# Normalising P and splitting it into f16 halves in two parts of eight heads, each turned by a transposing DMA of its own

## The chip, the cores and the metric

The kernel runs on one core of a Trainium2 chip. The metric is the device time of one execution in microseconds (us), lower is better, and the time of a kernel is the median of its runs. The engines are called PE (TensorE), DVE (VectorE), ACT (ScalarE), POOL (GpSimd) and SP (SyncE, which here only issues DMAs). They run side by side, each through its own list of instructions in order, and wait for each other through semaphores.

## What is computed

The input `x` is 64 sequences of 64 tokens with 512 features, with one condition vector of 512 per sequence. Four layers are added to it one after the other. The first is the one that the change touches:

```python
xn = _rms_norm(x, g_norm) * (1.0 + scale) + shift
q, k, v = split(xn @ W_qkv)                   # 16 heads of 32
q, k = _rms_norm(q, g_q), _rms_norm(k, g_k)
logits = jnp.einsum('bhqd,bhkd->bhqk', q, k) * d ** (-0.5)
attn = jax.nn.softmax(logits, axis=-1)        # this is P
o = jnp.einsum('bhqk,bhkd->bhqd', attn, v)
x = x + o + o @ W_out
```

The second layer samples `x` at 512 positions given by the condition (two taps with weights), the third is a GRU over the 64 tokens, the fourth an oscillator (four Runge-Kutta steps for each token) driven by the result.

## The kernel before, in words

The kernel has two stages. The first, attention and sampling, takes about 620 us, the second, the two recurrences side by side, the rest. The change is in the first stage alone.

**The slots.** The 64 sequences are taken in 32 pairs, so that the 128 tokens of a pair fill the 128 partitions. A software pipeline runs over slots `i = 0 to 31`: in slot i PE projects pair i to q, k and v (`project(p, 0)`, `(p, 1)` and `(p, 2)`, L1163), makes the scores of pair i-1 (`scores`, L1187), multiplies P with V for pair i-2 (`mix`, L1241) and projects that with `W_out` (`proj`, L1253), samples pair i-3 (`sample`, L1205) and turns the input of pair i+2 (L1262, L1264). A slot on PE starts with `turn_qk` (L1141). The order of every engine's work is written by hand in a function `slot` of its own; there is no scheduler.

**The way of P.** The scores of a pair lie in PSUM as 128 queries by 16 heads by 64 keys. In the slot after its projection a pair goes through these steps:

1. DVE takes the row minimum `mn` (L841), ACT makes 16 exponentials into `S`, one for each head, each with its row sum into `den` (`exps`, L515, 128x64 each).
2. DVE inverts the sums (`invert_sum`, L860: `rden` from `den`).
3. POOL multiplies `S` with `rden` (`norm_p`, L432, 128x1024).
4. ACT writes the high f16 half of `S` into `halves` (`high_halves`), POOL the rest as the low half (`low_halves`, L437). `halves` is a view of the tensor `front`, and the trace shows it under that name.
5. SP issues one transposing DMA from `halves` to `PT` (`turn_p`, L317), keys on the partitions.
6. `mix` in PE's next slot waits for it (`pt_in`).

The first two pairs make their exponentials in one instruction. The last two pairs, N1 and N0, are turned by PE instead of a DMA (L1173), after the same `invert_sum` and `norm_p`.

**What stands around it.** On DVE `invert_sum` stands behind `scale_qk` (L824, `qn`) and two of the eight `build` instructions of a slot (L795, `room<-rows,lidx`: an f16 compare that makes a selection matrix for `sample`), and ahead of `residual` (L888), `low_v` (L830), two `weigh_taps` (L863) and `low_wr` (L909). On ACT the order is `exps`, `high_v` (`Vt<-psQ`), `high_wr` (`Whh<-room` or `room<-room`, in most slots), `high_halves`. On POOL `norm_p` and `low_halves` end the slot, and the next one begins with `modulate` (L453, twice). On SP the transposing DMA is followed by the loads of x and of a row (L285, L289). In the trace buffer numbers are left out, so `first4` of the code is `first`. A helper `a` records all of ACT's work, so its line is L515 throughout.

## Time and profile before

| | us |
|---|---|
| median of 3 runs | 1564.39 |
| lowest and highest | 1557.45 and 1566.65 |
| the profiled execution | 1563.98 |
| its span, the part that the trace covers | 1562.2 |
| first stage, start of the span to the last sampling | about 632 |

Slots are given by their start on PE, which is the start of `turn_qk`. From 107.45 us, when the pipeline is full, to 581.09 us there are 26 of them, and they take 473.64 us. A busy time of an engine counts an instruction from its start to its end, so that an instruction that is held up by something inside the chip counts as busy while it is held.

### The profile page before, as it was taken

The numbers are of one execution on the slowest core, as the hardware profiler recorded it, in microseconds if no ns is written. First come the engines' busy times: TensorE is split into PE (matmuls) and PEld (weight loads), VectorE is DVE, ScalarE is ACT, GpSimd is POOL, SyncE is SP. The second block draws the span as 40 slices with busy tenths as digits, with TensorE's granted clock in tenths as the row PEclk, the third lists the DMA queues.
The fourth block names the chain that finished last, engine by engine and source line by source line (L and its number), as shares of the span: only waits on it lengthen the run. The fifth ranks groups of instructions, "written<-read, shape, count | busy, mean of one in ns | idle before, by whom it ended". The sixth has DMA issues, their size and how long they took to land.

```text
span 1562.2 us, 95585 instructions
## 1 busy us (share of the span) xinstructions
PE 1497.6 (96%) x42219; PEld 1327.1 (85%) x42219; DVE 1363.3 (87%) x3259; ACT 942.4 (60%) x2854; POOL 750.1 (48%) x887
## 2 busy tenths in 40 slices
PE   6899999999999999899999999999999999999995
PEld 3467776666667767899999999999999999999995
DVE  7889889888888889498888989988999889988997
ACT  6667777767777764355555555555555555555553
POOL 2566666666666665443433343433434343434331
PEclk8999999999999999999999999999999999999996
DMA  6333333444444434000000000000000000000000
GB/s 226 57 81 95 88 84 83 96 101 100 103 109 100 83 65 130 10 12 15 15 13 14 15 15 13 13 15 15 14 13 15 15 15 13 13 15 14 14 13 15
DMA packets 169054, 75.56 MB, mean 48 GB/s; under 512 B 139768, under 2 KB 154272, under 8 KB 168640
## 3 DMA queue, kind: packets, MB, share of 16 engines
q1 hardware_dynamic: 168544, 69.44, 19.4%
q8 instruction: 331, 5.42, 1.5%
q14 instruction: 83, 0.68, 0.1%
q10 hardware_dynamic: 96, 0.02, 0.0%
HBM read 33.71 MB, written 11.60 MB: 29 GB/s over the span
## 4 chain that ended last, share of the span: by engine, by line
PE 82%; DVE 5%; ACT 4%; issue 3%; POOL 3%; DMA 2%; ACTq 0%; POOLq 0%; DVEq 0%
PE psB L1472 34%; PE psA L1501 15%; PE psQ L1163 10%; PE psA L1506 7%; PE psQ L1205 6%; PE psO L1253 4%; DMA PT<-front 2%; ACT S L515 2%; PE psO L1241 2%; PE psB L1187 1%; PE psA L1141 1%; POOL S L432 1%; POOL front L437 1%; ACT front L515 1%; DVE room L795 1%
## 5 line engine op out<-in xcount | busy, mean ns | idle before, releaser
L1472 PE MATMUL psB<-first,Wx 128*128 128x64 f16 x9216 | 293.5, 194 | 5.5 <-POOL first L1784 3.8
L1501 PE MATMUL psA<-ts,Cp 128*128 128x64 f16 x8160 | 283.8, 194 | 10.3 <-ACT ts L1539 10.0
L1472 PE MATMUL psB<-first,Whh 128*128 128x64 f16 x9072 | 286.4, 193 | 0.8
L1472 PEld LDWEIGHTS psB<-first,Wx 128*128 128x128 f16 x9216 | 280.7, 98 | 6.7 <-POOL first L1784 3.9
L1163 PE MATMUL psQ<-Wx,front 128*128 128x512 f16 x1152 | 269.4, 384 | 6.3 <-DVE front L970 4.1
L1472 PEld LDWEIGHTS psB<-first,Whh 128*128 128x128 f16 x9072 | 273.8, 98 | 1.6 <-issue 1.6
L1539 ACT ACTIVATE ts<-qst 128x256 f16<-128x256 f32 x192 | 80.1, 417 | 313.9 <-DVE qst L1643 313.9
L1501 PEld LDWEIGHTS psA<-ts,Cp 128*128 128x128 f16 x8160 | 258.7, 99 | 11.5 <-ACT ts L1539 11.0
L1163 PEld LDWEIGHTS psQ<-Wx,front 128*128 128x128 f16 x1152 | 108.8, 99 | 126.7 <-issue 8.1
L1780 POOL TENSOR_TENSOR en<-rz,dn 128x256 f32<-128x256 f32 x64 | 46.8, 731 | 255.8 <-issue 255.6
L1506 PE MATMUL psA<-ts,Cp 128*128 128x64 f16 x4080 | 163.4, 194 | 0.7 <-issue 0.2
L795 DVE TENSOR_SCALAR room<-rows,lidx 128x512 f16<-128x512 f16 x256 | 158.0, 659 | 0.2 <-issue 0.2
L1506 PEld LDWEIGHTS psA<-ts,Cp 128*128 128x128 f16 x4080 | 138.6, 99 | 1.4 <-issue 1.2
L432 POOL TENSOR_TENSOR S<-S,rden 128x1024 f32<-128x1024 f32 x32 | 61.0, 1905 | 157.6 <-DVE rden L860 157.6
L1670 DVE TENSOR_TENSOR ts<-psA,ts 128x256 f16<-128x256 f32 x255 | 107.1, 420 | 31.7 <-ACT psA L1539 26.3
L515 ACT ACTIVATE S<-psB,mn 128x64 f32<-128x64 f32 x448 | 133.2, 338 | 0.6 <-DVE mn L841 0.4
L1643 DVE SCALAR_TENSOR_TENSOR rest<-cub,psQ 128x256 f32<-128x256 f32 x256 | 106.3, 415 | 7.0 <-DVE cub L1674 0.5
L1780 POOL TENSOR_TENSOR V<-X3b,first 128x256 f32<-128x256 f32 x64 | 47.0, 735 | 134.1 <-DVE first L1764 133.9
L1205 PE MATMUL psQ<-x,room 128*128 128x128 f16 x1856 | 108.5, 219 | 0.0
L1643 DVE SCALAR_TENSOR_TENSOR psO<-qst,psO 128x256 f32<-128x256 f32 x256 | 106.5, 416 | 0.0
L1205 PEld LDWEIGHTS psQ<-x,room 128*128 128x128 f16 x1856 | 104.9, 98 | 0.2
L515 ACT ACTIVATION_READ_ACCUMULATOR S<-psB,mn 128x1 f32 x448 | 104.0, 232 | 0.0
(201 smaller groups left out, 3001.0 us busy)
## 6 DMA issues: line engine op xcount, KB each, us to landing
front<-in_x SPq DMA_DIRECT2D x32, 256.0 KB, 4.6
rows<-rows_dram SPq DMA_DIRECT2D x64, 128.0 KB, 3.1
out<-ot SPq DMA_DIRECT2D x512, 16.0 KB, 1.8
x<-x SPq DMA_DIRECT2D x29, 224.0 KB
Whh<-in_L_cond_W_qkv SPq DMA_DIRECT2D x12, 256.0 KB, 7.2
room<-in_L_cond_W_hh SPq DMA_DIRECT2D x12, 256.0 KB, 2.7
room<-in_L_cond_W_ih SPq DMA_DIRECT2D x12, 256.0 KB, 2.8
wih_dram<-room SPq DMA_DIRECT2D x12, 256.0 KB, 3.2
```

Of the source, the lines that this page charges most:

```text
L432: nc.gpsimd.tensor_tensor(S[:, :, :], S[:, :, :], rden[:, :].unsqueeze(2).broadcast_to([PART, HEADS, T]), ALU.mult)\
L515: return nc.scalar.activation(out, in_, f, **k)
L795: e = v.tensor_scalar(E_of(p, b)[:, k, :], rows[b][:, :], lidx[:, k:k + 1], None, ALU.is_equal)
L1163: last = mm(psQ[:, n, :], xn[p.u][:, i, c, :], Wqkv[:, j, c, n * D:(n + 1) * D], start=(c == 0 and t == 0), stop=(c == KC - 1 and t == 2))
L1205: last = mm(o[:, m, :, :], E_of(p, b)[:, c, m * PART:(m + 1) * PART], x1_of(p)[:, :, i, c, b, :], start=(c == 0 and i == 0), stop=(c == KC ...
L1472: last = mm(o, W_[:, i, c, g * PART:(g + 1) * PART], src[:, j, c, :], start=False, stop=False, skip_group_check=True)
L1501: mm(psF[:, s % 2, m, :], Cp[:, i, c, m * PART:(m + 1) * PART], ts_[:, 0, c, :], start=(c == 0 and m == 0 and i == 0), stop=False, skip_gr ...
L1506: last = mm(psF[:, s % 2, m, :], Cp[:, 0, c, m * PART:(m + 1) * PART], ts_[:, 1, c, :], start=False, stop=(c == KC - 1), skip_group_check= ...
L1539: return nc.scalar.activation(out, in_, f, **k)
L1643: return v.scalar_tensor_tensor(out=flat(out), in0=flat(in0), scalar=scalar, in1=flat(in1), op0=ALU.mult, op1=op1)
L1670: v.tensor_tensor(ts_[:, 1, :, :], th, ts_[:, 0, :, :], ALU.subtract).then_inc(S["ts_ready"], 1)
L1780: return nc.gpsimd.tensor_tensor(flat(out), flat(in0), flat(in1), op)
```

## The change

`S`, `halves` and `PT` are treated as two parts of eight heads (h = 0 and 1). `halves` and `PT` are laid out part by part, so that one part is contiguous in each partition, and `mix` reads the new layout. Each of `norm_p`, `low_halves`, `high_halves`, `invert_sum` and `turn_p` becomes two instructions of half the width, with two counts of its semaphore for each pair in place of one. A new semaphore `exp_half` is counted up by the eighth exponential. On DVE the inversion of the first eight sums moves ahead of the last two `build` instructions and waits for `exp_half`; on ACT the first part's `high_halves` moves ahead of `high_v`. The number of matmuls stays.

```diff
         def turn_p(p, h):
-            sp.wait_ge(pl_done, p.n + 1)
+            sp.wait_ge(pl_done, p.n * 2 + h + 1)
             need(sp, mix_done, p.n)
-            sp.dma_start_transpose(PT[:, :, :, :].rearrange("p i j n -> p (i j) n"), halves.rearrange("p i s k -> p (i s k)"))\
+            sp.dma_start_transpose(PT[:, h, :, :, :].rearrange("p i j n -> p (i j) n"), halves[:, h, :, :, :].rearrange("p i s k -> p (i s k)"))\
                 .then_inc(pt_in, 16)
...
         def norm_p(p):
-            pool.wait_ge(rden_done, p.n + 1)
-            nc.gpsimd.tensor_tensor(S[:, :, :], S[:, :, :], rden[:, :].unsqueeze(2).broadcast_to([PART, HEADS, T]), ALU.mult)\
-                .then_inc(p_done, 1)
+            for h in range(2):
+                pool.wait_ge(rden_done, p.n * 2 + h + 1)
+                part = S[:, 8 * h:8 * h + 8, :]
+                nc.gpsimd.tensor_tensor(part, part, rden[:, 8 * h:8 * h + 8].unsqueeze(2).broadcast_to([PART, HEADS // 2, T]), ALU.mult)\
+                    .then_inc(p_done, 1)
...
         def low_halves(p):
-            pool.wait_ge(ph_done, p.n + 1)
-            nc.gpsimd.tensor_tensor(halves[:, 1, :, :], S[:, :, :], halves[:, 0, :, :], ALU.subtract).then_inc(pl_done, 1)
+            for h in range(2):
+                pool.wait_ge(ph_done, p.n * 2 + h + 1)
+                nc.gpsimd.tensor_tensor(halves[:, h, 1, :, :], S[:, 8 * h:8 * h + 8, :], halves[:, h, 0, :, :], ALU.subtract).then_inc(pl_done, 1)
...
-        def high_halves(p):
-            act.wait_ge(p_done, p.n + 1)
-            need(act, pt_in, p.n * 16)
-            a(halves[:, 0, :, :], S[:, :, :]).then_inc(ph_done, 1)
+        def high_halves(p, h):
+            act.wait_ge(p_done, p.n * 2 + h + 1)
+            need(act, pt_in, p.n * 32)
+            a(halves[:, h, 0, :, :], S[:, 8 * h:8 * h + 8, :]).then_inc(ph_done, 1)
...
-        def invert_sum(p):
-            dve.wait_ge(exp_done, p.n + 1)
-            need(dve, p_done, p.n)
-            v.reciprocal(rden[:, :], den[:, :]).then_inc(rden_done, 1)
+        def invert_sum(p, h):
+            if h == 0 and p.n in range(2, N1.n):
+                dve.wait_ge(exp_half, p.n - 1)
+            else:
+                dve.wait_ge(exp_done, p.n + 1)
+            need(dve, p_done, p.n * 2)
+            v.reciprocal(rden[:, 8 * h:8 * h + 8], den[:, 8 * h:8 * h + 8]).then_inc(rden_done, 1)
...
             if p := pair(-1):
                 if p.n < 2:
                     sum_p(p)
-                invert_sum(p)
+                    invert_sum(p, 0)
+                invert_sum(p, 1)
```

DVE, the end of a slot before (`room1` is the matrix that `build` writes, `XR` the running x):

```order
231 L824 TENSOR_TENSOR qn<-psQ,rs 128x512 [waits qk_T,rs_step]
232 L824 TENSOR_TENSOR qn<-psQ,rs 128x512
233 L795 TENSOR_SCALAR room1<-rows1,lidx 128x512 x2
234 L860 RECIPROCAL rden<-den 128x16 [waits p_done,exp_done]
235 L888 SCALAR_TENSOR_TENSOR XR<-psO,XR 128x4x64 [waits xT_kept,proj_done]
```

And now:

```order
238 L833 TENSOR_TENSOR qn<-psQ,rs 128x512 [waits qk_T,rs_step]
239 L833 TENSOR_TENSOR qn<-psQ,rs 128x512
240 L872 RECIPROCAL rden<-den 128x8 [waits p_done,exp_half]
241 L804 TENSOR_SCALAR room1<-rows1,lidx 128x512 x2
242 L872 RECIPROCAL rden<-den 128x8 [waits p_done,exp_done]
243 L900 SCALAR_TENSOR_TENSOR XR<-psO,XR 128x4x64 [waits xT_kept,proj_done]
```

The first reciprocal now stands ahead of the two compares, with a wait for the first eight exponentials only; the second stands where the one stood.

ACT, from the exponentials to the end of a slot before (`Whh` is `high_wr`'s target, `front<-S` is `high_halves`):

```order
125 L515 ACTIVATE S,den<-psB,mn 128x64 [waits pl_done,mn_done]
126 L515 ACTIVATE S,den<-psB,mn 128x64 x13
127 L515 ACTIVATE Vt0<-psQ 128x512 [waits mix_done,qkv_done]
128 L515 ACTIVATE Whh<-room0 128x512 [waits wr_in0]
129 L515 ACTIVATE front<-S 128x1024 [waits pt_in,p_done]
130 L515 ACTIVATE rsB<-psB 128x128 [waits xr_done,xy_T]
```

And now:

```order
126 L519 ACTIVATE S,den<-psB,mn 128x64 [waits pl_done,mn_done]
127 L519 ACTIVATE S,den<-psB,mn 128x64 x13
128 L519 ACTIVATE front<-S 128x512 [waits pt_in,p_done]
129 L519 ACTIVATE Vt0<-psQ 128x512 [waits mix_done,qkv_done]
130 L519 ACTIVATE Whh<-room0 128x512 [waits wr_in0]
131 L519 ACTIVATE front<-S 128x512 [waits pt_in,p_done]
132 L519 ACTIVATE rsB<-psB 128x128 [waits xr_done,xy_T]
```

The first part's copy moved ahead of `Vt` and `Whh`, and the wait for POOL (`p_done`) moved with it.

## Rows read from the trace of the kernel before

**Rows 1.** The page, busy time of each engine over the span.
```profile
PE 1497.6 (96%) x42219; PEld 1327.1 (85%) x42219; DVE 1363.3 (87%) x3259; ACT 942.4 (60%) x2854; POOL 750.1 (48%) x887
```

**Rows 2.** Length; busy us PE, PEld, DVE, ACT, POOL; clock; DMA: 12 long slots.
```profile
125.14:143.53 18.39, 18.10 (x356) 12.83 (x355) 17.31 (x29) 13.46 (x50) 12.95 (x12) 1.00 0.36 89
...
sum 223.56, PE 214.54 PEld 153.53 DVE 202.83 ACT 161.84 POOL 152.85; mean PE 17.88 PEld 12.79 DVE 16.90 ACT 13.49 POOL 12.74
```

**Rows 3.** The same view, the 14 short slots: the first, and the sum.
```profile
107.45:125.14 17.69, 17.63 (x355) 12.77 (x354) 14.99 (x29) 13.50 (x50) 11.28 (x11) 1.00 0.36 92
...
sum 250.08, PE 247.55 PEld 177.99 DVE 215.23 ACT 187.80 POOL 161.43; mean PE 17.68 PEld 12.71 DVE 15.37 ACT 13.41 POOL 11.53
```

**Rows 4.** Waits, 60 to 600 us: waiter, releaser, us in total, times, longest.
```profile
DVE rden L860 <- ACT S L515: 25.0, 28, 1.4
...
PE psO L1241 <- DMA PT<-front: 5.4, 6, 1.6
...
PE psQ L1163 <- issue: 2.1, 2, 1.1
```

**Rows 5.** PE in order of time, a long slot: start, us, idle before.
```profile
406.47 1.20 PE L1241 MATMUL psO<-PT,Vt 64*32 64x64 f16 x96 [1.01 <-DMA PT<-front]
```

**Rows 6.** SP in order of time: two of the 30 transposing DMAs.
```profile
308.89 1.89 SPq L317 DMA_TRANSPOSE PT<-front  x1
...
400.36 2.72 SPq L317 DMA_TRANSPOSE PT<-front  x1
```

**Rows 7.** Line L317: from issue to landing, all 30.
```profile
DMA to landing us min/median/max: 4.3/4.7/6.1
```

**Rows 8.** DMA, 308 to 316 us in 40 slices of 0.2 us: busy tenths, GB/s.
```profile
DMA  0000000000299999999999999776423322322000
GB/s 0 0 0 0 0 0 0 0 0 0 55 212 225 210 204 214 219 219 216 218 216 183 253 255 184 195 266 246 143 67 108 97 72 97 108 97 87 5 0 0
```

**Rows 9.** POOL in order of time, 303 to 318 us.
```profile
303.65 1.90 POOL L432 TENSOR_TENSOR S<-S,rden 128x1024 f32<-128x1024 f32 x1 [5.08 <-DVE rden L860]
306.73 2.13 POOL L437 TENSOR_TENSOR front<-S,front 128x1024 f16<-128x1024 f32 x1 [1.17 <-ACT front L515]
308.82 1.09 POOL L453 TENSOR_TENSOR front<-front,modA 128x512 f32<-128x512 f32 x1
...
315.98 1.15 POOL L460 TENSOR_TENSOR front<-front 128x512 f16<-128x512 f32 x1
```

**Rows 10.** ACT in order of time, the last two exponentials and what follows.
```profile
302.52 0.38 ACT L515 ACTIVATE S<-psB,mn 128x64 f32<-128x64 f32 x1
...
302.81 0.39 ACT L515 ACTIVATE S<-psB,mn 128x64 f32<-128x64 f32 x1
...
303.10 0.68 ACT L515 ACTIVATE Vt<-psQ 128x512 f16<-128x512 f32 x1
303.58 0.72 ACT L515 ACTIVATE Whh<-room 128x512 f16<-128x512 f32 x1
305.59 1.06 ACT L515 ACTIVATE front<-S 128x1024 f16<-128x1024 f32 x1 [1.29 <-POOL S L432]
```

**Rows 11.** DVE in order of time, around the same pair's sums.
```profile
301.54 0.60 DVE L795 TENSOR_SCALAR room<-rows,lidx 128x512 f16<-128x512 f16 x2
303.32 0.25 DVE L860 RECIPROCAL rden<-den 128x16 f32<-128x16 f32 x1 [1.18 <-ACT S L515]
...
307.81 1.19 DVE L795 TENSOR_SCALAR room<-rows,lidx 128x512 f16<-128x512 f16 x1
```

**Rows 12.** DVE in order of time, the slot after.
```profile
320.77 0.25 DVE L860 RECIPROCAL rden<-den 128x16 f32<-128x16 f32 x1 [0.22 <-ACT S L515]
...
326.13 0.34 DVE L795 TENSOR_SCALAR room<-rows,lidx 128x512 f16<-128x512 f16 x1
```

**Rows 13.** The chain that ended last, 600 to 612 us.
```profile
605.58 0.27 DVE rden L860
...
605.92 1.91 POOL S L432
```

More of the change, by code:

```diff
@@ L143, in attention_and_sampling @@
     rsB = sb("rsB", [PART, PART])
-    halves = front[:, 2:4, :].rearrange("p v n -> p (v n)").bitcast(F16).rearrange("p (i s k) -> p i s k", i=2, k=T)
+    halves = front[:, 2:4, :].rearrange("p v n -> p (v n)").bitcast(F16).rearrange("p (h i s k) -> p h i s k", h=2, i=2, k=T)
     xa = front[:, 4, :].rearrange("p (c b t) -> p c b t", c=KC, b=2)
@@ L157, in attention_and_sampling @@
     rden = sb("rden", [PART, HEADS])
[L158 removed]
+    PT = sb("PT", [PART, 2, 2, KC, PART], F16)
     oT = sb("oT", [PART, 2, KC, PART], F16)
@@ L336, in slot @@
             if p := pair(-2):
-                turn_p(p)
+                turn_p(p, 0)
+                turn_p(p, 1)
             if p := pair(3):
@@ L606, in exps @@
                       accum_out=den[:, s:s + 1])
+                if s == HEADS // 2 - 1:
+                    e.then_inc(exp_half, 1)
             if hi == HEADS:
@@ L688, in slot @@
                     exps(p, 2, HEADS)
+                    high_halves(p, 0)
                 else:
@@ L698, in slot @@
             if p := pair(-1):
-                high_halves(p)
+                if p.n < 2:
+                    high_halves(p, 0)
+                high_halves(p, 1)
         act.wait_ge(cond_T, 1)
@@ L1030, in slot @@
                 low_cp(0)
+            if (p := pair(-1)) and p.n > 1:
+                invert_sum(p, 0)
             if tap:
@@ L1035, in slot @@
                     sum_p(p)
-                invert_sum(p)
+                    invert_sum(p, 0)
+                invert_sum(p, 1)
             if p := pair(-2):
@@ L1095, in _ @@
         sum_p(N1)
-        invert_sum(N1)
+        invert_sum(N1, 0)
+        invert_sum(N1, 1)
         residual(N2)
@@ L1104, in _ @@
         sum_p(N0)
-        invert_sum(N0)
+        invert_sum(N0, 0)
+        invert_sum(N0, 1)
         low_o(N1)
@@ L1167, in turn_p @@
         def turn_p(p):
-            pe.wait_ge(p_done, p.n + 1)
+            pe.wait_ge(p_done, p.n * 2 + 2)
             need(pe, qk_ready, NP)
@@ L1228, in mix @@
                 if p.n <= N2.n:
-                    pe.wait_ge(pt_in, 16 * (p.n + 1))
+                    pe.wait_ge(pt_in, 32 * (p.n + 1))
                 else:
@@ L1242, in mix @@
                                   Vt[p.u][rows_, i, h * DH:(h + 1) * DH],
-                                  PT[rows_, k, r // 2 * KC + c, (r % 2) * T:(r % 2 + 1) * T], start=(t == 0), stop=(t == 2))
+                                  PT[rows_, r // 2, k, c, (r % 2) * T:(r % 2 + 1) * T], start=(t == 0), stop=(t == 2))
             last.then_inc(mix_done if b else mix0_done, 1)
```

15 lines of the change are left out of this document (7 added, 8 removed).

## The prediction

> **What bounds the kernel now.** I read the page first: PE is busy 96% of the span and DVE 87% [rows 1], so PE is the bound and DVE stands close behind. The change can only shorten the time by what PE loses around it, so the next view is the busy time by stretch, one stretch for each slot on PE. It shows two kinds of slot that mostly alternate. Fourteen short ones take 250.08 us, 17.86 on average, with PE busy in 17.68 of it; the best, at 17.69, has no hole worth the name [rows 3]. Twelve long ones take 223.56 us, 18.63 on average [rows 2]. The reader should look at DVE's column: 16.90 us in a long slot against 15.37 in a short one, and POOL's, 12.74 against 11.53, for the same instructions. TensorE's granted clock is 1.00 in these rows, its upper level, so the clock plays no part in the difference. Against 26 slots at 17.69 (459.9), the 473.64 us hold 13.7 us that PE loses. The list of waits names 5.4 us of loss as PE waiting for the transposing DMA, six times, at most 1.6 us each [rows 4]; 1.6 of it is in the slot that starts at 66 us, before the 26, and 3.8 in them. A wait of 1.01 us in a long slot is shown in [rows 5]; its DMA was issued at 400.36 [rows 6] and `mix` started 6.1 later, the longest landing of the 30 [rows 7].
>
> Why long and short? POOL and DVE tell it. In the slot that starts at 288.84 the inversion runs at 303.32, after 1.18 us of waiting for ACT's exponentials [rows 11]; POOL then multiplies 303.65 to 305.55, ACT makes the high half 305.59 to 306.65, POOL the low half 306.73 to 308.86 [rows 9, 10], and the DMA goes at 308.89 [rows 6]. The next slot began at 306.70, so POOL's low half runs into it: DVE's compare of 307.81 lasts 1.19 us and ends when POOL's does [rows 11], while the same compare in the slot after takes 0.34 [rows 12]. Late P in one slot thus makes the next one long, through DVE. The Trainium skill, page "SBUF — State Buffer", section "SBUF: two separate sides", says that DVE in its fast modes and GpSimd take a shared port pair as an exclusive lock for a whole instruction; the 1.19 against 0.34 agrees.
>
> **The change part by part.** I follow the pair of [rows 9 to 11].
> - *Inversion.* One reciprocal of 0.25 us becomes two, priced at 0.25 each (less than nothing is excluded, it is one instruction more; 0.25 is the upper end as each is narrower). The first stands at 301.54, where the compares start now [rows 11]. Does its new wait for eight exponentials stop DVE and the compares, `residual`, `low_v` queued behind it? The last of sixteen started at 302.81 and they come 0.29 us apart [rows 10], so the eighth started near 300.5 and was done by 301. No wait.
> - *Product.* POOL started 0.33 us after the reciprocal [303.32 to 303.65, rows 9, 11], so the first part runs from 301.87. A half has 128x512 elements; the nearest row is the 128x512 multiply with `modA`, 1.09 us [rows 9], against 0.95 for half of 1.90. I take 1.09: ends 302.96. The second starts at 303.65 as before and ends 304.74. The pair costs POOL 0.3 more, but 1.1 of it moves into its idle 5.08 us.
> - *High half on ACT.* Nearest row for 128x512 is `Vt`, 0.68 us; two are 1.36 in place of 1.06. Part 0 starts when the exponentials end, 303.10, its product done at 302.96: no wait. `Vt` and `Whh` behind it slide by 0.6, to about 303.7 and 304.3 [rows 10]; their readers on DVE, `low_v` and `low_wr`, come behind the 1.3 us of `residual`, so cover is there. Where the exponentials end early, as before the reciprocal of 320.77 with its wait of only 0.22 [rows 12], ACT waits for POOL some 0.5 us more. ACT is busy 13.5 us of an 18 us slot [rows 2, 3], so I cost that at nothing. Part 1 starts at about 305.0, ends 305.7, a microsecond before the present 306.65.
> - *Low half on POOL.* Nearest row: 128x512 to f16, 1.15 us [rows 9]. Part 0 runs 304.74 to 305.89, part 1 to 307.04, in place of 308.86: **1.8 us earlier**, though the two cost 0.2 more.
> - *Transposing DMA.* The 2.4 us of full activity in [rows 8] are its transfer; of the median 4.7 us to landing [rows 7], 2.3 are fixed. A half should land in 2.3 + 1.2 = 3.5 (bounds: 2.3, no transfer, and 4.7, no cheaper than a whole). Issue took 1.89 us for a whole [rows 6]; halves take 0.95 if by size, 1.9 if not. Part 0 is issued near 305.9, so its issue is over by 307.8 at worst; part 1 then lands between 307.04 + 3.5 = 310.5 and 307.8 + 4.7 = 312.5, against 313.6 now. The loads of x and rows behind it on SP move earlier or at worst stay. In the slices of [rows 8] before the transfer the DMA engines stand idle, so nothing new collides.
> - *PE.* It needs P 7.3 us into a slot; even the 6.1 us landing, from 307.8, gives 313.9 against the present start of `mix`, about 314.0. The wait of 5.4 us [rows 4] should go in all but a stray case.
> - *DVE.* Two opposed effects. Against: the second compare of 301.54 would now meet POOL's first product and be held until it ends, 302.96, so the pair ends at about 303.0 in place of 302.1. In that slot DVE then waits until 303.32 anyway, so 0.9 + 0.25 us lie in its 1.18 of idle time: nothing. Where only 0.22 is idle [rows 12] up to 0.9 shows on DVE. For: the compare of 307.81 finds POOL's low half gone and falls from 1.19 to 0.34, and what follows it shifts up.
> - *The end.* The last pair's product stands alone in the chain, 1.91 us behind a reciprocal of 0.27 [rows 13]. In two parts it is 2 x 1.09 for 1.91: 0.3 us lost, 0.5 with the reciprocal.
>
> **The sum.** With P early in every slot the cause of the long slots goes, and the 12 become short: 12 x (18.63 - 17.86) = 9.2 us. Two of the long ones, however, contain PE stalls at a projection that wait for nothing in the trace, 2.1 us together [rows 4]; they stay: 7.1. Add the 1.6 us wait at the start, take off 0.4 for the end: 8.3 us. The profiled execution took 1563.98, so 1555.7; against the median, 0.4 higher, 1556.1. **Forecast 1556 us.** Its own bounds: 1553 if half of what the short slots still lose (14 x 0.17 and more) goes as well, 1559 if it is the waits alone.
>
> **A rule that speaks against it.** The Trainium skill, "DMA: Bandwidth & Descriptors", section "Rules for kernel authors", wants small transfers coalesced into a large one, and gives mostly overhead below 64 KB. A part here is far above that. If the rule held fully and the fixed part ran twice in a row, it is the second rival below.
>
> **The rivals.**
> 1. *Only the named waits go.* The DMA is early, but DVE's held compares merely move from the slot's start to its end, so long slots stay long without their DMA wait. For: the port conflict is moved, not removed [rows 11, 12]. Against: at the end of a slot DVE mostly has idle time. 1564.4 - 5.4 + 0.4 = 1559.4.
> 2. *The halves land no earlier.* If the second DMA is served only after the first has landed, in 2 x 3.5 = 7.0 us from 305.9, it lands at 312.9, and with two stray landings of the long kind it is where it was. The change then does not do what it says, and the parts' overhead remains: 1564 to 1566. For: no row shows two such DMAs together. Against: the transfer is half of the landing, so the rest can overlap.
> 3. *DVE becomes the bound: slower.* The first product always holds the second compare, 0.9 us, and the extra reciprocal costs 0.25. If DVE has under 1.15 us to spare ahead of the second reciprocal in every slot, `residual`, `weigh_taps`, then `low_qk` and the next scores come late by the rest. The point from which it decides is this idle time: 25.0 us in 28 waits, 0.9 each [rows 4], nearly covers it, 0.22 as in [rows 12] would not. If half of it shows in each of 28 slots, 28 x 0.58 = 16 us, minus 5.4 for the waits, 1575; all of it, 1591. Against: each slot that gets short has, like that of [rows 11], 1.18 idle.
> 4. *More than 1% faster.* All 13.7 us of loss, the 1.6 and some of the pipeline's filling go: under 1549. It needs the stalls without a cause to vanish too.
>
> **How the numbers follow.** Forecast 54%, rival 1 18%, rival 2 14%, rival 3 8%, rival 4 6%. A measurement of this kernel tells about 1% (15.6 us) from no change; its own runs before lie 9 us apart. Faster by over 1% is rival 4 and nothing of the others, 6%; slower by over 1% is the upper part of rival 3, 6%; the rest, 88%, is within. The range, leaving out most of rivals 3 and 4: 1549 to 1567.
>
> **What the changed profile would show.** Right: no DMA among PE's releasers, or under 1 us; 26 slots of about 17.9 without alternation, 465 us together; part 1's DMA issued under 0.6 us into the slot and landing under 4.5; the compare at a slot's start 0.34 us nearly always, the one behind the first reciprocal about 1. Rival 1: the same, with long slots at 18.2. Rival 2: landings of 5 and more from the second issue. Rival 3: the second reciprocal no longer waits for ACT, and PE waits for DVE at L1187. I would be wrong above all if the first compare got the port and POOL's product came so late that ACT, waiting ahead of `Vt`, passes the delay on to DVE.

## The result and the profile after

| | before | after |
|---|---|---|
| median of 5 runs, us | 1559.94 | 1548.35 |
| lowest and highest | 1557.45 and 1566.65 | 1545.15 and 1551.52 |
| the profiled execution | 1563.98 | 1551.52 |
| its span | 1562.2 | 1549.7 |
| the 26 slots of the full pipeline | 473.64 | 465.30 |

The ratio is 0.9911, with an interval of 0.989 to 0.9932: a small gain that is certain in its sign, near 1%. The forecast was 1556 with a range down to 1549; the time lies 0.65 us below that end.

The two profiled executions lie 12.5 us apart. I split them by stretch, since the stages share nothing but their ends:

- the three slots in which the pipeline fills: 60.52 to 55.78, 4.7 less
- the 26 full slots: 473.64 to 465.30, 8.3 less
- the slot behind them, in which the pipeline begins to drain: 11.50 to 11.37, 0.1 less
- what follows, the products of the last pair and the second stage, of which the change touches only the first: 969.61 to 970.22, 0.6 more

The page after, busy time by engine:

```profile
PE 1492.9 (96%) x42219; PEld 1321.8 (85%) x42219; DVE 1393.2 (90%) x3291; ACT 946.1 (61%) x2884; POOL 759.6 (49%) x949
```

Against [rows 1] PE has the same matmuls and 4.7 us less of busy time, while DVE is busy 29.9 us more, with 32 instructions more. Reciprocals, 64 of 0.19 for 32 of 0.25, make 4.2 of it. Most of the rest is time in which DVE's instructions are held: in the 26 full slots the compares take 153.5 us in place of 130.4 and `low_wr` 35.6 in place of 15.8, while a small step of the norm (`ms`, L813) falls from 19.1 to 9.0. It is the first thing to see: the change made DVE "busier" and the kernel faster.

The busy time by stretch (columns as in [rows 2]), a full slot and all 26:

```profile
102.81:120.70 17.89, 17.76 (x355) 12.68 (x354) 17.29 (x30) 13.51 (x51) 12.40 (x13) 1.00 0.38 91
102.81:568.11 465.30, 461.07 (x9176) 329.19 (x9174) 446.94 (x752) 353.34 (x1321) 322.89 (x338) 1.00 0.40 94
```

The alternation of [rows 2, 3] (17.69 and 18.4) is gone: 24 of the 26 slots take 17.87 to 18.00, and DVE is busy 17.3 to 17.5 us of nearly all of them. These 24 are the slots that follow a `low_wr`. The last two, which follow none, take 17.69 and 17.20 (18.09 and 17.60 before), so PE can do less than 17.9. The waits (60 to 600 us: waiter, releaser, us in total, times, longest):

```profile
DVE rden L872 <- ACT S L519: 1.0, 3, 0.4
```

No DMA stands among PE's releasers, where it had 5.4 us, and DVE's idle time ahead of the reciprocal, 25.0 us before [rows 4], is 1.0. DVE still waits for ACT ahead of `ss` (L826), 10.9 us in 28 waits. DVE in order of time, in the pair's slot that answers to [rows 11]:

```profile
312.97 0.19 DVE L872 RECIPROCAL rden<-den 128x8 f32<-128x8 f32 x1
313.08 1.35 DVE L804 TENSOR_SCALAR room<-rows,lidx 128x512 f16<-128x512 f16 x2
314.35 0.19 DVE L872 RECIPROCAL rden<-den 128x8 f32<-128x8 f32 x1
...
316.91 1.55 DVE L921 SCALAR_TENSOR_TENSOR room<-room 128x512 f16<-128x512 f32 x1
...
319.58 0.34 DVE L804 TENSOR_SCALAR room<-rows,lidx 128x512 f16<-128x512 f16 x1
```

And POOL in the same stretch:

```profile
313.24 1.04 POOL L435 TENSOR_TENSOR S<-S,rden 128x512 f32<-128x512 f32 x1 [3.09 <-DVE rden L872]
314.62 1.05 POOL L435 TENSOR_TENSOR S<-S,rden 128x512 f32<-128x512 f32 x1 [0.34 <-DVE rden L872]
315.63 2.28 POOL L441 TENSOR_TENSOR front<-S,front 128x512 f16<-128x512 f32 x2
...
319.74 1.09 POOL L457 TENSOR_TENSOR front<-front,modA 128x512 f32<-128x512 f32 x1 [1.83 <-DVE front L788]
```

Three things are to be read off these two lists. The compares of 313.08 take 1.35 us for two instead of 0.60: the second starts into POOL's first product and ends just after it. The compare of 319.58, the first of the next slot, is free, 0.34. And `low_wr` (L921), which took 0.68 before, now starts 316.91 inside POOL's two low halves (315.63 to 317.91) and ends 0.55 us after them: 1.55 us. The 23 of the full slots take 1.55 us on average. In "SBUF — State Buffer" (section "SBUF: two separate sides"), the Trainium skill counts a DVE instruction with two SBUF inputs among those that must have the shared pair to themselves, against a POOL instruction that reads SBUF. `low_wr` has two such inputs, and the trace agrees. DVE's `um` (L875, 316.31), with one input in SBUF and one in PSUM, ran inside the same low halves and took 0.68 us, as everywhere.

The transposing DMAs on SP (start, us, count), their landing, and the `mix` that waits for them:

```profile
298.82 2.65 SPq L317 DMA_TRANSPOSE PT<-front  x2
```
```profile
DMA to landing us min/median/max: 3.1/3.2/5.1
```
```profile
307.22 1.20 PE L1258 MATMUL psO<-PT,Vt 64*32 64x64 f16 x96
```

The first is issued at 298.82 and lands at 302.08, the second is issued at 300.21 and lands at 303.29. P is there 3.9 us before PE wants it, in place of arriving with it or late. (The text on record of the first experiment, below, says 302.1 and five microseconds: it took the first part's landing for the second's.)

The filling of the pipeline gave 1.6 us a slot, more than any full slot did. Before:

```profile
46.93:66.16 19.23, 16.33 (x293) 10.41 (x294) 14.89 (x25) 10.39 (x22) 12.02 (x9) 0.91 0.31 61
66.16:87.94 21.78, 18.25 (x360) 13.20 (x359) 16.43 (x33) 13.88 (x50) 11.56 (x10) 1.00 0.37 74
87.94:107.45 19.51, 17.84 (x356) 12.69 (x355) 18.57 (x34) 13.57 (x50) 12.49 (x12) 1.00 0.34 84
```

After:

```profile
47.03:65.02 17.99, 14.87 (x296) 9.76 (x295) 15.13 (x27) 10.31 (x22) 12.26 (x11) 1.00 0.39 64
65.02:84.54 19.52, 18.05 (x360) 13.12 (x359) 16.89 (x34) 14.11 (x52) 13.61 (x14) 1.00 0.35 86
84.54:102.81 18.27, 17.77 (x356) 12.68 (x355) 18.03 (x34) 13.61 (x51) 12.44 (x13) 1.00 0.36 87
```

In the same stretch (46 to 108 us) PE waits for DVE's `low_qk`, first before, then after:

```profile
PE psB L1187 <- DVE first L774: 5.5, 3, 2.6
```
```profile
PE psB L1204 <- DVE first L783: 3.4, 2, 2.0
```

In the first of these slots TensorE's granted clock was 0.91 before and 1.00 after: before, some 3.4 us of it ran at the lower level, 1.2 GHz, and the projection in them took 3.81 us instead of 2.76. That could be 1.05 us of luck in this pair of executions. A second profile of the changed kernel (below), in which the clock fell there too, settles how much of the 4.7 is the change's.

### The profile page after: what moved, and what is told of

It reads as the page before. It is cut to its first block, busy times and chain, and to the rows that moved or that the text cites. A ratio compares the mean times of both kernels' runs of the same rounds, so it can differ in the third digit from the quotient of the medians.

```text
span 1549.7 us, 95828 instructions
## 1 busy us (share of the span) xinstructions
PE 1492.9 (96%) x42219; PEld 1321.8 (85%) x42219; DVE 1393.2 (90%) x3291; ACT 946.1 (61%) x2884; POOL 759.6 (49%) x949
## 4 chain that ended last, share of the span: by engine, by line
PE 89%; DVE 5%; issue 2%; ACT 1%; POOL 1%; ACTq 0%; POOLq 0%; DVEq 0%
PE psB L1489 35%; PE psA L1518 15%; PE psQ L1180 13%; PE psA L1523 8%; PE psQ L1222 7%; PE psO L1270 5%; PE psB L1204 2%; PE psA L1158 2%; DVE room L804 1%; PE psO L1258 1%; PE psB L1279 1%; DVE ss L826 1%; ACT front L519 1%; DVE oT L893 1%; POOL S L435 0%
## 5 line engine op out<-in xcount | busy, mean ns | idle before, releaser
L1518 PE MATMUL psA<-ts,Cp 128*128 128x64 f16 x8160 | 283.3, 193 | 12.0 <-ACT ts L1556 10.9
L804 DVE TENSOR_SCALAR room<-rows,lidx 128x512 f16<-128x512 f16 x256 | 182.2, 754 | 0.2
L435 POOL TENSOR_TENSOR S<-S,rden 128x512 f32<-128x512 f32 x64 | 66.6, 1043 | 121.9 <-DVE rden L872 121.9
```

The costliest lines, as they stand in the source:

```text
L804: e = v.tensor_scalar(E_of(p, b)[:, k, :], rows[b][:, :], lidx[:, k:k + 1], None, ALU.is_equal)
L1518: mm(psF[:, s % 2, m, :], Cp[:, i, c, m * PART:(m + 1) * PART], ts_[:, 0, c, :], start=(c == 0 and m == 0 and i == 0), stop=False, skip_gr ...
```

## The experiments

The prediction held P's earlier arrival for the cause of everything, and left open which of the three edits brings it: two DMAs, the early first reciprocal, or the halves as such. In the texts on record "26 slots" is the stretch shown above. Ratios are to the kernel before on the same chip, with their interval. After each kernel stands its row of the 26 slots (start and end, length, busy us PE, PEld, DVE, ACT, POOL, clock, DMA).

**One DMA for the pair.** The changed kernel, with P turned whole.

```diff
-            sp.wait_ge(pl_done, p.n * 2 + h + 1)
+            sp.wait_ge(pl_done, p.n * 2 + 2)
-            sp.dma_start_transpose(PT[:, h, :, :, :]..., halves[:, h, :, :, :]...)
+            sp.dma_start_transpose(PT[:, :, :, :, :]..., halves[:, :, :, :, :]...)
```

> The changed kernel with one transposing DMA for each pair, issued when both parts' low halves are done; product and halves stay in two parts. In the changed kernel the second part landed at about 302.1 us and the product with V began at 307.2, so five microseconds are to spare. Theory A (the gain is the early product and early low halves, which leave the port that DVE and POOL share free when the next slot begins; the DMA has slack): a landing 1.2 to 1.5 us later costs nothing, 26 full slots again take about 465 us, ratio to the kernel before 0.989 to 0.993. Theory B (the halved transfer is what ended PE's waits): slots become uneven again, ratio 0.995 to 0.998.

Ratio 0.9936 (0.9916 to 0.9956), median 1552.05.

```profile
104.50:570.02 465.52, 461.06 (x9176) 329.38 (x9174) 447.26 (x752) 353.40 (x1321) 323.05 (x338) 1.00 0.39 94
```

The ratio lies just above theory A's range, the slots are as it said: the full slots don't notice the second DMA, 465.52 against 465.30. What comes back is one wait in the second filling slot, where a whole P is late (PE in order of time):

```profile
75.70 1.20 PE L1257 MATMUL psO<-PT,Vt 64*32 64x64 f16 x96 [1.47 <-DMA PT<-front]
```

The filling takes 57.59 (46.91 to 104.50), against 55.78 in the changed kernel and 56.06 in its second profile. So dividing the DMA is worth 1.5 to 1.8 us, all of it while the pipeline fills.

**The two DMAs alone.** The kernel before, with its halves laid out by part and turned by two DMAs, both behind the one `low_halves`.

```diff
             sp.wait_ge(pl_done, p.n + 1)
             need(sp, mix_done, p.n)
-            sp.dma_start_transpose(PT[:, :, :, :]..., halves...)
+            for h in range(2):
+                sp.dma_start_transpose(PT[:, h, :, :, :]..., halves[:, h, :, :, :]...)
```

> The kernel before with only its transposing DMA in two (one behind the other, both after the whole low half); reciprocal, product and halves undivided. Theory A: P is as late as before, POOL's low half still runs into the next slot, so the alternation stays; at best PE's named waits of 5.4 us shrink: ratio 0.996 to 1.001. Theory B (two DMAs land earlier, 3.3 against 4.7 us, and that is the gain): 0.990 to 0.993.

Ratio 1.002 (1.0 to 1.0039), median 1566.57: no gain, and slightly above the range of theory A.

```profile
106.84:579.58 472.74, 460.82 (x9176) 331.77 (x9174) 416.89 (x725) 349.13 (x1295) 314.42 (x287) 1.00 0.40 93
```

Its waits and its landings:

```profile
PE psO L1243 <- DMA PT<-front: 9.8, 16, 1.5
```
```profile
DMA to landing us min/median/max: 3.1/3.3/5.0
```

The median over all 60 hides that the two parts differ. The first lands in 3.3 us; the second is issued 1.3 us behind it, and 20 of the 30 second parts take 4.2 to 5.0 us to land. So P is complete later than with one DMA, and PE waits for it longer, 9.8 us against 5.4. Together with the first experiment this shows that the DMA isn't where the full slots' gain comes from.

**Both reciprocals behind the compares.** The changed kernel, with the first reciprocal back beside the second.

```diff
-            if (p := pair(-1)) and p.n > 1:
-                invert_sum(p, 0)
             if tap:
                 build(tap, 1, (2, 3))
             if p := pair(-1):
                 if p.n < 2:
                     sum_p(p)
-                    invert_sum(p, 0)
+                invert_sum(p, 0)
                 invert_sum(p, 1)
```

> The changed kernel with the first reciprocal behind the two compares, next to the second, where the one reciprocal stood before. Theory A': DVE now has nearly no idle time (17.3 of 17.9 us in a slot), and its second compare is held 0.7 us by POOL's first product; with the reciprocal behind, the compares take 0.6 us in place of 1.35, DVE gets 0.7 us a slot back, P comes 0.3 us later, which nothing waits for: slots go from 17.9 towards 17.7, ratio to the kernel before 0.986 to 0.991. Rival: the early start of the product is itself the gain; then slots become long and short again and the ratio goes to 0.994 or more.

Ratio 0.9969 (0.9954 to 0.9985), median 1557.43: slower than the changed kernel, the reverse of theory A'. The rival had the sign, but not the even slots.

```profile
102.97:575.68 472.71, 461.23 (x9175) 329.38 (x9174) 443.11 (x752) 352.39 (x1321) 322.56 (x339) 1.00 0.39 93
```

The early reciprocal alone is worth 7.4 us in the full slots (472.71 against 465.30), where I had put it down as a cost. Without it the changed kernel gains in the filling only: its 472.71 stand against 473.64 before, of which 2.1 were stalls without a releaser. DVE, and ACT between its lines, show why:

```profile
319.84 0.69 DVE L839 TENSOR_TENSOR Vt<-psQ,Vt 128x512 f16<-128x512 f32 x1 [0.48 <-ACT Vt L519]
...
321.05 1.58 DVE L921 SCALAR_TENSOR_TENSOR room<-room 128x512 f16<-128x512 f32 x1
```
```profile
318.69 0.63 ACT L519 ACTIVATE front<-S 128x512 f16<-128x512 f32 x1 [1.10 <-POOL S L435]
```

ACT's first copy now stands ahead of `Vt` and waits 1.10 us for POOL's late product; DVE's `low_v` waits 0.48 for `Vt`; and `low_wr` is held as well, 1.58. This is the mishap that the prediction named last. The 24 slots that follow a `low_wr` all take 18.22 to 18.27, the last two 17.69 and 17.18, and no wait for P's DMA is among PE's in them. What PE waits for is DVE's `oT`, ahead of the product with `W_out` (L1268), 9.3 us in 25 waits. An early P is therefore not enough to make a slot short.

**The same, with ACT's first copy behind `Vt`.**

```diff
                     exps(p, 2, HEADS)
-                    high_halves(p, 0)
...
             high_v(pair(0))
+            if (p := pair(-1)) and p.n > 1:
+                high_halves(p, 0)
```

> The kernel with both reciprocals behind the compares (as in e2_inv_behind), and on ACT the first part's high half behind Vt's copy in place of ahead of it. In e2_inv_behind ACT waited 1.10 us for POOL's first product ahead of Vt's copy, and DVE waited 0.48 us for that copy in each slot; 26 full slots took 472.7 us against 465.3. Theory D (DVE is the bound of a slot now, so every wait that it takes over counts in full): without that wait a slot falls from 18.24 to 17.7 or 17.8, 26 slots take 460 to 464 us, ratio to the kernel before 0.987 to 0.991. Rival (the early start of the product is what counts, whatever DVE waits for): slots stay at 18.2, ratio 0.996 to 0.998.

Ratio 0.9938 (0.9918 to 0.9957), median 1550.51: 4.3 us less in the slots than the kernel that it mends (the intervals of the two ratios touch), not as good as I expected, and not what the rival said either.

```profile
102.91:571.36 468.45, 459.76 (x9176) 329.49 (x9174) 420.78 (x751) 351.91 (x1321) 327.22 (x339) 1.00 0.39 94
```

Slots alternate between 17.7 and 18.3 again, and `low_wr` alternates with them. Where it takes 0.84 to 0.91 us, the next slot takes 17.69 to 17.75; where it takes 1.54 to 1.56, the next takes 18.26 to 18.43. The exceptions are a slot of 19.43 with a PE stall of 1.57 us without a releaser in it, and the one behind it (17.76).

**The kernel before, with its first compare behind `low_qk`.** If the held first compare [rows 11] makes the long slots, moving it away from POOL's low half should cure them.

```diff
-            if tap and tap.n > 0:
-                build(tap, 0, (0,))
             if p := pair(-1):
                 low_qk(p, 0)
                 low_qk(p, 1)
             if tap:
-                build(tap, 0, (1, 2, 3) if tap.n > 0 else range(KC))
+                build(tap, 0, range(KC))
```

> The kernel before with the first of DVE's compares of a slot moved behind low_qk, so that POOL's late low half can hold no work ahead of the next scores. Theory A: long slots lose the 1.2 us compare ahead of the scores, but the compares behind are held by POOL in its place, so some of the 8 us come back: ratio 0.994 to 0.999, PE's waits for the DMA stay. Rival C (the long slots have another cause than the compare): 1.000 within 0.002.

Ratio 1.002 (1.0002 to 1.0038), median 1564.98. My theory missed.

```profile
107.95:581.62 473.67, 461.68 (x9175) 331.55 (x9174) 419.45 (x725) 352.11 (x1295) 313.82 (x286) 1.00 0.39 93
```

The slots are as uneven as before, 17.71 to 18.98 (the last one, 17.56, aside), so the held first compare isn't what makes them long. The low half holds a compare behind `low_qk` in its place: the compares of the 26 slots take 125.7 us against 130.4. And DVE now waits 0.59 us in each slot for ACT's `first`, which the compare had covered.

**Where PE loses the time.** The starts of PE's groups tell at which step a slot is late. In the short slot of the kernel before that starts at 325.02, PE starts the scores 3.55 us in, the second projection at 4.46, `mix` at 7.15, the third projection at 8.28, the product with `W_out` at 10.88, and the next slot begins 6.81 later. What 25 full slots (the last one is shorter) take over these distances, in us:

| | to the end of the scores | ahead of `mix` | in `mix` | ahead of `W_out` | behind it | sum |
|---|---|---|---|---|---|---|
| before | 1.9 | 6.6 | 3.2 | 1.8 | 0.2 | 13.7 |
| its first compare moved | 1.0 | 6.0 | 3.7 | 2.9 | 0.1 | 13.8 |
| both reciprocals behind | 0.0 | 0.0 | 0.2 | 12.8 | 0.2 | 13.2 |
| changed | 0.0 | 0.0 | 0.0 | 5.5 | 0.2 | 5.8 |

So a late low half lengthens a slot of the kernel before in several ways. P lands late: 3.9 us of the 6.6 are named waits for it, and 2.1 the stalls without a releaser. The compare ahead of `low_qk` is held, which tells on the scores; moved, it gave back 0.9 us, and the product with `W_out` lost 1.1. That product waits for DVE's `oT`, and the way to it is over POOL's own list: `modulate` starts when the low half ends, 2.12 us into the long slot of 306.70 [rows 9] and 1.28 into the short one behind it. POOL's last conversion (L460) then ends 10.43 us into the slot [rows 9] against 9.60, and holds the two compares ahead of `oT`, which take 1.57 us against 0.60. The pauses in `mix`, up to 0.7 us in a slot, have no releaser in the trace. They are gone in the changed kernel, but also in the kernel before with two DMAs (0.0), where P is as late, so why they come isn't known.

Late low halves and long slots go together. In 11 of the 25 slots `modulate` starts later than 1.8 us, and they take 18.18 to 19.11; the other 14 take 17.69 to 17.97, except four of 18.01 to 18.37 with a pause in or ahead of `mix`. The alternation follows: the low half ends 5.5 us after the reciprocal, which stands 14.1 us into this long slot and 14.4 into this short one, so a long slot lets it end early in the next one, and a short slot late. This is read from the traces; no run tests it alone.

**More work on DVE, in both kernels.** A reduction of 0.69 us on DVE ahead of `low_v`. If DVE's own work bounds the changed kernel, each slot grows by it; the kernel before has 25 us of idle time to take it.

```diff
             dve.wait_ge(v_hi, p.n + 1)
+            v.tensor_reduce(spare[:, :], psQ[:, 2, :], AX.X, ALU.add)
             v.tensor_tensor(Vt
```

> The changed kernel with one more DVE instruction of some 0.6 to 0.7 us in each slot, a reduction of V's PSUM bank into a spare column that nothing reads, ahead of low_v. Theory D (DVE has no slack left): each full slot grows by 0.5 to 0.65 us, 26 slots by 13 to 17, ratio to the kernel before 1.000 to 1.004. Rival (PE is the bound and DVE has a half microsecond to spare): growth under 0.2 a slot, ratio 0.991 to 0.995.

> The kernel before with the same additional DVE instruction at the same place. DVE waits there 25 us for the exponentials and others, so if that idle time is real slack at this place, slots grow by 0.1 to 0.3 us, ratio 1.001 to 1.005, clearly less than the same instruction costs the changed kernel. If the long slots of before were also bound by DVE, the long ones grow by the full 0.6 and the ratio is 1.006 or more.

The changed kernel with it: ratio 0.9941 (0.992 to 0.9962), median 1551.74. The kernel before with it: 1.0037 (1.0019 to 1.0055), median 1565.47. Their 26 slots, in this order:

```profile
103.71:571.35 467.64, 461.20 (x9175) 329.16 (x9174) 447.28 (x778) 353.33 (x1321) 322.99 (x338) 1.00 0.38 94
```
```profile
107.96:585.75 477.79, 462.86 (x9175) 332.27 (x9174) 442.99 (x752) 349.76 (x1295) 325.22 (x287) 1.00 0.38 92
```

The kernel before grew by 0.16 a slot, or 0.18 without the stalls that wait for nothing (1.60 us here, 2.1 before), as expected. For the changed kernel I had expected 13 to 17 us and got 2.3, of which 1.8 are PE stalls without a releaser. That is the rival's number, and theory D fell; the next experiment shows that the rival's reason, PE as the bound, doesn't hold either. Apart from five slots the length is the same as without the reduction. DVE's busy time tells where 26 x 0.69 = 18 us went: 447.28 against 446.94, none of it there. `low_wr` takes 13.7 us less, the compares 3.9. The rows show it, first DVE, then POOL:

```profile
318.26 0.69 DVE L840 TENSOR_REDUCE spare<-psQ 128x1 f32<-128x512 f32 x1
...
320.06 0.94 DVE L923 SCALAR_TENSOR_TENSOR room<-room 128x512 f16<-128x512 f32 x1
```
```profile
318.17 2.28 POOL L442 TENSOR_TENSOR front<-S,front 128x512 f16<-128x512 f32 x2
```

`low_wr` started 0.6 us later relative to POOL's low halves, and took 0.94 instead of 1.55. Its end lies 0.55 us behind the end of POOL's second low half in the changed kernel, here, and in the kernel with both reciprocals behind: POOL sets it, not its own start. So DVE's busy 17.4 us are not 17.4 us of work, and the limit is a loop over two engines: first reciprocal, POOL's products and low halves, release of `low_wr`, the rest of DVE's slot, the next reciprocal.

The trace of the changed kernel closes this loop, and shows that its second half runs over POOL's list again, as above. In the slot that starts at 318.04, `low_wr` is released at 318.46, DVE's `front` follows (318.98) and lets POOL begin `modulate` at 319.74. DVE, POOL and PE then:

```profile
326.88 1.57 DVE L804 TENSOR_SCALAR room<-rows,lidx 128x512 f16<-128x512 f16 x2
```
```profile
326.89 1.15 POOL L464 TENSOR_TENSOR front<-front 128x512 f16<-128x512 f32 x1
```
```profile
329.11 2.85 PE L1270 MATMUL psO<-oT,Wo 128*128 128x128 f16 x48
```

POOL's conversion holds the compares ahead of `oT`, and PE's product with `W_out` starts 11.07 us into the slot, late at the one step at which the changed kernel loses time. The next first reciprocal comes at 330.85, 17.88 us after the one of 312.97: the length of the slot. DVE's idle time ahead of `ss`, 0.39 us in this slot, lies beside the loop and not in it.

**`low_wr` out of POOL's way.** That loop is cut where `low_wr` meets the low halves: it is done one slot later, ahead of the first reciprocal. All else as in the changed kernel.

```diff
             if i == 0:
                 low_cp(0)
+            if 0 <= i - 1 - WR_FROM < WR_PIECES:
+                low_wr(i - 1 - WR_FROM)
             if (p := pair(-1)) and p.n > 1:
                 invert_sum(p, 0)
...
-            if 0 <= i - WR_FROM < WR_PIECES:
-                low_wr(i - WR_FROM)
             if tap:
                 weigh_taps(tap, 1)
```

> The changed kernel with low_wr taken one slot later and put on DVE just ahead of the first reciprocal, where POOL is idle. In the changed kernel it takes 1.55 us a slot where it took 0.69 before, since POOL's low half runs beside it; 24 slots have it. Theory D (DVE is the bound of a slot, and the held low_wr costs it 0.87): 24 of 26 slots fall from 17.93 towards PE's own 17.69, so some 5 us less, 26 slots take about 460 us, ratio 0.985 to 0.989. Rival (PE's loss of 0.2 us a slot has another cause): no change, 0.991, or worse, since P comes 0.6 us later.

Ratio 0.9889 (0.9864 to 0.9914), median 1541.78.

```profile
102.96:563.38 460.42, 457.74 (x9175) 330.22 (x9174) 417.52 (x752) 355.19 (x1321) 323.26 (x338) 1.00 0.40 95
```

```profile
310.64 0.68 DVE L921 SCALAR_TENSOR_TENSOR Whh<-room,Whh 128x512 f16<-128x512 f32 x1
...
311.35 1.36 DVE L804 TENSOR_SCALAR room<-rows,lidx 128x512 f16<-128x512 f16 x2
```

`low_wr` is back at 0.68, DVE is busy 29.4 us less in the 26 slots with the same 752 instructions, and 23 of them take 17.69 to 17.75, the length of the short slots before [rows 3] (the others 17.80, 17.92 and, the last, 17.20). POOL's `modulate` starts 1.28 us into every slot, where it was 1.69 in the changed kernel, and ahead of PE's product with `W_out` 0.4 us are lost in 25 slots, not 5.5 (0.9 in all, not 5.8). The loop was the limit, and PE is the bound again. The compares behind the first reciprocal are still held (1.36), `ms` is held for 1.0 us a slot, and neither costs anything.

**Is the early reciprocal needed then?** The same kernel, with both reciprocals behind the compares (the edit of the experiment on the early reciprocal).

```diff
-            if (p := pair(-1)) and p.n > 1:
-                invert_sum(p, 0)
             if tap:
                 build(tap, 1, (2, 3))
             if p := pair(-1):
                 if p.n < 2:
                     sum_p(p)
-                    invert_sum(p, 0)
+                invert_sum(p, 0)
                 invert_sum(p, 1)
```

> low_wr moved as in e6_wr_moved, and both reciprocals behind the compares as in e2_inv_behind. Theory F (what sets a slot of the changed kernel is a loop of POOL and DVE: first reciprocal, products, low halves, release of the held low_wr, the rest of DVE's slot, next reciprocal; an earlier reciprocal shortened that loop by 0.28 us a slot and counts for nothing once low_wr stands elsewhere): slots stay at PE's own 17.7, 26 slots at 460 to 462 us, ratio to the kernel before 0.987 to 0.991. Rival (the early product itself keeps slots short): slots of 18 and more, 26 slots over 465 us, ratio 0.994 or more.

Ratio 0.9912 (0.9885 to 0.9939), median 1549.59, a hair above the range.

```profile
103.03:563.37 460.34, 457.67 (x9175) 329.95 (x9174) 400.61 (x752) 354.93 (x1321) 323.49 (x339) 1.00 0.41 95
```

In the slots it makes no difference, 460.34 against 460.42: the 7.4 us of the early reciprocal were the price of a loop that is no longer closed. The whole time doesn't tell the two apart, the intervals overlap. The second stage, the same instructions at a granted clock of 0.990 and 0.993, took 978.74 us in this execution and 964.05 in the one above (first the kernel with the early reciprocal, then this one):

```profile
574.75:1538.80 964.05, 935.18 (x31498) 929.88 (x31498) 849.41 (x2364) 518.29 (x1365) 380.98 (x546) 0.99 0.09 17
```
```profile
574.76:1553.50 978.74, 944.24 (x31498) 934.23 (x31498) 850.98 (x2364) 517.84 (x1365) 381.27 (x546) 0.99 0.09 17
```

No kernel of this study changes that stage, and its length varies by more than most of the gains here.

**`low_wr` moved in the kernel before.** The same move without the division of P.

```diff
             if i == 0:
                 low_cp(0)
+            if 0 <= i - 1 - WR_FROM < WR_PIECES:
+                low_wr(i - 1 - WR_FROM)
             if tap:
                 build(tap, 1, (2, 3))
...
-            if 0 <= i - WR_FROM < WR_PIECES:
-                low_wr(i - WR_FROM)
```

> The kernel before with low_wr alone moved as in e6_wr_moved. There POOL is idle while low_wr runs, so it is not held. Theory F: the low half still runs into the next slot and P still comes late for PE, so nothing is gained: ratio 0.998 to 1.003, 26 slots 470 to 476 us, PE's waits for the DMA stay. Rival (the place of low_wr is worth the same without the parts): 0.990 to 0.995.

Ratio 0.9997 (0.9982 to 1.0012), median 1563.35.

```profile
107.33:576.88 469.55, 461.34 (x9175) 331.01 (x9174) 418.60 (x726) 349.76 (x1295) 314.79 (x287) 1.00 0.39 93
```

The whole gains nothing that can be told. The 26 slots take 4.1 us less, just under the range on record, but 2.1 of that are the stalls without a releaser, which this execution didn't have, and the uneven kernels are known by one profile each. PE's waits for P are still there, 2.5 us in three. In the slots the two moves nearly add up, 8.3 and 4.1 alone and 13.2 together, of the 13.7 that PE lost; that they need each other isn't shown.

**Both kernels again.** The changed kernel and the one with `low_wr` moved, unaltered, beside the kernel before on one chip, since one profile of each carried the argument.

```diff
(no edit)
```

> The changed kernel once more, beside the next one on one chip: ratio to the kernel before 0.989 to 0.994, 26 slots 465 us.

> e6_wr_moved once more beside the changed kernel on one chip: 26 slots 460 us, 0.002 to 0.005 of the ratio below that of the changed kernel. If the two come out equal, the 5 us seen in the slots are given back elsewhere.

Ratios 0.9928 (0.9904 to 0.9952), median 1552.52, and 0.9894 (0.9871 to 0.9916), median 1547.26. Their 26 slots:

```profile
104.55:569.99 465.44, 461.08 (x9175) 329.25 (x9174) 447.12 (x752) 353.36 (x1321) 322.94 (x338) 1.00 0.40 94
```
```profile
104.64:564.88 460.24, 457.64 (x9175) 330.20 (x9174) 417.52 (x752) 354.87 (x1321) 323.28 (x338) 1.00 0.40 95
```

The slots repeat to 0.2 us. The filling of both took 56.06 us (48.49 to 104.55 for the changed kernel), against 60.52 in the kernel before, and 60.07 to 60.95 in the four kernels made from it. In these two the clock fell in the first filling slot as it had before (0.91), and the projection took 4.45 us. It cost 0.3 us against the first profile, since PE waited less behind it. So 4.5 of the 4.7 us belong to the change, and the clock isn't the explanation.

## Why the prediction was right in its sign and short in its size

**What held.** The change made P early, and the alternation of long and short slots went. PE's waits for the DMA went. The 26 slots were to take 465 and take 465.30. In the chain of DVE, the compare behind the first reciprocal is held (1.35 for two, forecast: the pair from 301.54 to 303.0, 1.5), and the one at the slot's start is free, 0.34. The halves cost POOL 1.04 and 1.05 for the products (1.09 forecast), 2.28 for both low halves (2.30), ACT 0.63 and 0.62 (0.68), each reciprocal 0.19 (0.25). Rival 2 fell: two parts of one pair land in 3.2 us each (3.5 forecast), the second issued before the first has landed, and one DMA in their place was 1.5 us worse while the pipeline fills. The forecast took 2.4 us of full activity from [rows 8], where 14 slices, 2.8 us, stand at nine tenths; it made no difference. The end was to cost 0.4; the chain of waits has 2.21 us for the last pair's reciprocal and product, against 2.18 [rows 13], so it cost next to nothing:

```profile
592.09 0.17 DVE rden L872
592.26 2.04 POOL S L435 x2
```

In sum, of the 8.3 forecast for the pair of executions and the 12.5 measured: the start 3.1 more than forecast, the full slots 1.2 more, the end and the last slot 0.5 more, the second stage 0.6 less.

That the full slots came out at the forecast 17.9 is in part luck. The 17.86 of the forecast was the average of the short slots before, with what late P cost them; the 17.93 of the changed kernel is set by the hold of `low_wr`, which the forecast didn't have.

**The step that failed: "Add the 1.6 us wait at the start".** The filling of the pipeline gave 4.7 us, and 4.5 in the second profile, in which the clock was as before. There the 4.5 can be read from PE's idle time: the wait for the DMA is gone, 1.6 as forecast; the waits for DVE's `low_qk` fell from 5.5 to 3.2, which is 2.3; small ones give 0.5. I had counted the one wait that had a DMA's name on it, and left out `low_qk`, though it stood in the same stretch. Half of the 2.3 is one hold: in the third filling slot the late low half (87.44 to 89.58) held a one-off DVE instruction ahead of `low_qk`, and PE waited 1.16 us there. The waits for `low_qk` in the second profile (48.4 to 104.6 us), then the one-off instruction before and after:

```profile
PE psB L1204 <- DVE first L783: 3.2, 2, 2.2
```
```profile
88.19 1.41 DVE L983 TENSOR_TENSOR brz<-vT 128x8 f32<-128x8 f32 x1
```
```profile
84.79 0.16 DVE L995 TENSOR_TENSOR brz<-vT 128x8 f32<-128x8 f32 x1
```

Of the terms of the sum this one was mis-sized most.

**The stalls that were to stay.** "They stay: 7.1" instead of 9.2: the 2.1 us of projections that waited for nothing weren't in this profile of the changed kernel, nor in nine of the twelve that followed, while three have 1.6 to 1.9 us of them. They come and go between executions. Taking them off was no finding about the change. With them left out on both sides, the full slots gave 6.2 us (471.5 to 465.3), less than the 7.1 of the forecast; the 8.3 has 2.1 us of luck in it.

**"With P early in every slot the cause of the long slots goes".** The outcome came, and late low halves and long slots do go together, but the compare by which the prediction linked them is the smaller part (1.9 of 13.7 us, at the scores): with it out of POOL's way the kernel before got no faster. The waits for P and POOL's own delayed list count as well. Nor is an early P sufficient. With both reciprocals behind the compares P is early too, and the slots are 18.2, for ACT waits ahead of `Vt`, DVE behind it, and `low_wr` is released later. What made them 17.9 is the early first reciprocal, 7.4 us, which I had priced as harmless and not as a gain.

**DVE: "nothing".** Here the forecast was right for the wrong reason. I let DVE's idle 25.0 us swallow the held compare, and expected the rest to remain idle. In fact it was used up entirely, to 1.0, by a hold that I hadn't looked for: POOL's low halves, 1.8 us earlier, fell onto `low_wr`. I had put `low_wr` among the readers of ACT that have cover, and asked only whether it starts late, not what runs on POOL while it does. That hold set the slot at 17.9 where PE could do 17.7, and cost the change 5 us that it could have had.

**The base.** I set the change against the median of three runs, 1564.39; that of five is 1559.94. From there the same sum, 8.3 less, gives 1551.6, and the remaining 3.3 us are the terms above. The base, 4.4 us, is the greater part of the miss. The low end of the range, 1549, was built from slots and stalls, and took no account that the second stage alone moves by several us from one execution to the next. The time fell where rival 4 had it, under 1549, but not by what rival 4 said: of the 13.7 us that PE lost in the full slots, 5.4 are still there.

**What stays open.** How the long slots of the kernel before share out among their causes is read from the traces and was not tested by a run of its own. Why `mix` pauses in them. Where PE's stalls without a releaser come from, and why the second stage takes 964 in one execution and 979 in another at a clock of 0.99 in both.

## What to carry to other kernels

Moving a POOL instruction earlier moves its hold on DVE onto other instructions: for each moved one, lay its new interval over DVE's list and look for what it falls on. DVE's busy share can't say whether it is the bound when such holds count as busy; adding a small instruction can: if the slot doesn't grow by it, DVE's own work isn't the bound. To find the way of a delay, lay the starts of the bounding engine's groups in a short and a long slot side by side: the step where the distance grows is the one to explain. And a wait named in the profile prices one cause only: in a pipeline that is still filling, look at every wait of the bounding engine, since it has no full slot to hide them in.

## What the hardware showed that I had not expected

- Held instructions end with POOL's or up to 0.55 us behind, whatever their start: `low_wr` took 0.68 us free, 0.94 when it started late in POOL's low halves, 1.52 to 1.60 when early. Small instructions are held as well: one on 128x33 elements took 0.18 to 1.22 us, one on 128x8 elements 0.16 free and 1.41 held.
- The transposing DMA of a half P (128x512, high and low) was issued in 1.3 us and landed 3.2 us from the start of its issue; the whole took 1.9 and 4.7. In the changed kernel the second of two, issued before the first had landed, took no longer than the first (medians 3.1 and 3.3). In the kernel before with two DMAs back to back, 20 of the 30 second parts took 4.2 to 5.0; why isn't known.
- Two executions of the same second stage differed by 14.7 us (964.05 and 978.74) at nearly equal granted clock (0.993 and 0.990), with PE's busy time 9.1 us apart for the same 31498 matmuls.
